# Attention over 16 images: keys' second half, means, values and maxima at other places in slots 0, 2, 4 and 6

## The chip, the cores and the metric

One core of one Trainium2 chip runs the kernel. The metric is the device time of one execution in microseconds (us). TensorE does the matrix products, VectorE (DVE in the rows), ScalarE (ACT) and GpSimd (POOL) the rest; SyncE (SP) issues the transfers.

## The reference

For each of 16 images `x` has 512 channels and 1024 positions. The reference is, without what doesn't matter here:

```python
q, k, v = split(einsum('bchw,oc->bohw', x, w_qkv), 3)   # 8 heads of 64
sim  = einsum('bhdi,bhdj->bhij', q * 64**-0.5, k)
out  = einsum('bhij,bhdj->bhid', softmax(sim), v)
y    = einsum('bchw,oc->bohw', out, w_out) + b_out
y    = y * rsqrt(mean(y*y, axis=channels) + 64**-0.5) * rms_scale
return y + x
```

All of it is in float32. The softmax is over the 1024 keys of each query.

## The kernel before, in words

**Slots and places.** One image is one batch of eight slots (0 to 7). A slot is a pair of heads and one half (512) of the queries. It goes through 16 places (`t`). At the even places TensorE makes the scores of one step of 128 keys for the two heads (`scores`, L741 and L750: four products of 512 columns, two for each head) and ScalarE makes their exponentials (L871). A head has one bank for its scores, so the next step's product of a head waits until the exponential of that head's last step is done (the wait on `prob_ready` in `scores`). The odd places hold everything else. `items_at` lists it: each item has a name and one of four auxiliary banks of PSUM (0 to 3).

**The items.** K0 and K1 are the two halves of the next head pair's keys, each twelve products of 512 columns (L584). ScalarE copies such an item twice (the high parts, L903), and then VectorE subtracts twice (the low parts, L1118), which frees the bank. V0 to V3 are values for later slots (24 products of 256 columns, L628), copied by ScalarE (L913). M00 to M31 are products of keys and queries from which VectorE takes maxima for the next slot (L726, reduced at L1125, L1131 and L1137): `maxima_of_tile` makes tile 0 and 1 at place 1, tile 2 and 3 at place 9; each tile claims banks 0 and 1, then 2 and 3. T transposes the maxima (L642), in the midst of Q, the next queries, at place 15. O0, O1 and P are the projection of the output (L657). R is the mean of squares of the batch before (L666, L667; slots 0 and 1 only): VectorE reads it at L1170.

**Place 9** also holds the values of steps 0 to 3 (`values`, L763, four products a step). `VALUES_FIRST[slot]` says how many of the four steps come ahead of tile 2; tile 3 comes behind all of them.

**Names for what is split.** x is held as a high part, made by ScalarE, and a remainder `x_lo` (`split_x`, L374). An image has eight pieces: 0 to 3 are the first half of the positions, 4 to 7 the second. The next batch's are split in slots 5 and 6. GpSimd makes the remainders of all pieces but number 6; VectorE makes that one at place 4 of slot 6 (`SPLIT_LOW_AT[6] = (6, 4)`, `SPLIT_BY = ((6,), ...)`). In slot 6 the keys are the next batch's. Their item begins with `wait_x(body, h)`: K0 (h = 0) waits for pieces 0 to 3, K1 (h = 1) for all eight, number 6 among them. V1 of slot 6 reads columns of the first half alone.

**Order.** Every engine's order is the order of the program. On VectorE, for each place: the items of the place, then at place 2 the reciprocals (L1183) and the normalisation (L1190), and last the split of x if the place has one. ScalarE makes the exponentials of an even place, then its items. `OUTPUT_HIGH_AT` is the place at which ScalarE makes the high part of the normalised output (L942); in slots 0 and 1 it waits for R, which uses the same buffer. GpSimd adds the exponentials (L1306) and makes the low part of the output at place 8 (L392).

**Ahead of the loop** a prologue (`PRO_ITEMS`) makes the first keys, queries, values and maxima. VectorE copies the mask and the negative identity there (L1246, L1247), ahead of the maxima of tile 1. The first batch has no R; in the last, slots 6 and 7 make no keys, values or queries for a next one.

Of the kernel before, what the change touches and what calls it, by code (L numbers as in the profile page):

```python
# [25 lines left out]

INVERT_SUMS_AT = ((2, 2),) * 8
NORMALISE_AT = (2,) * 8
OUTPUT_HIGH_AT = (4, 8, 8, 4, 8, 6, 4, 4)
OUTPUT_LOW_AT = 4  # L30

REPEAT_K_AT = (8, 9)
# [2 lines left out]
SPLIT_MAXIMA = (1, 3)  # L35


VALUES_FIRST = (2, 1, 0, 0, 0, 1, 2, 0)

# [7 lines left out]
SQUARE_AT = (((7, 14), (7, 14), (0, 0), (0, 0)), ((0, 14), (0, 14), (1, 0), (1, 0)))  # L49
ADD_SQUARES_IN = (0, 1)  # L50
SQUARES_HIGH_AT = ((0, 1), (1, 1))
MEAN_AT = ((0, 3), (1, 7))

INVERT_AT = (((0, 10), (0, 12), (0, 14), (1, 0)), ((1, 10), (1, 12), (1, 14), (2, 0)))
ROOT_AT = ((1, 0), (2, 0))
# [20 lines left out]
def items_at(slot, t, first, last):  # L76

    following = not (last and slot == SLOTS - 1)
    projected = not (last and slot >= SLOTS - SLOT_QUERIES)
    preceding = not (first and slot == 0)  # L80
    out = []
    if t in (1, 9) and following:
        for it in (0, 1) if t == 1 else (2, 3):
            out.append((f"M{it}0", 0))
            if it in SPLIT_MAXIMA:
                out.append((f"N{it}0", 1))
            out.append((f"M{it}1", 2))
    if t == 3 and slot in (0, 2, 4):
        out.append(("K0", 0))
    elif t == 3 and (slot in (1, 3) or slot == 6 and projected or slot == 7 and following):  # L90
        out.append(({1: "V0", 3: "V2", 6: "V1", 7: "V2"}[slot], 0))
    if t == 5 and slot == 6 and projected:
        out.append(("K0", 1))
    elif t == 5 and slot in (2, 4):
        out.append(("K1", 1))
    if LATE_OUTPUT.get(slot - 1) == t:
        out.append(("P", 0 if t == 3 else 2))
    if t == 7:
        if slot == 0:
            out.append(("K1", 1))  # L100
        elif slot in (1, 3):
            out.append((f"V{slot}", 1 if slot == 1 else 3))
        elif slot == 5 and not last:
            out.append(("V0", 3))
        elif slot == 6 and projected:
            out.append(("K1", 2))
        elif slot == 7 and following:
            out.append(("V3", 3))
    if (slot, t) in MEAN_AT and not first:
        out.append(("R", 2))  # L110
    if t == (11 if following else LAST_OUTPUT_AT) and preceding:
        out.append(("O0", 0))
    if t == (13 if following else LAST_OUTPUT_AT) and preceding and slot not in LATE_OUTPUT:
        out.append(("O1", 2))
    if t == 15:
        if following:
            out.append(("T", 0 if slot in LATE_OUTPUT else 2))
        if projected:
            out.append(("Q", 2 if slot in LATE_OUTPUT else 0))
    return out  # L120


def in_halves(slot, name):

    return name == {0: "K1", 1: "V1", 3: "V3", 5: "V0", 7: "V3"}.get(slot)


def output_item(slot, name):
# [26 lines left out]
def body_items(first, last):  # L155
    return [(s, n, k) for s in range(SLOTS) for t in range(PLACES) for n, k in items_at(s, t, first, last)]


def attention_kernel(nc, x, wqkv, wout, bias, scale, consts, out):
# [27 lines left out]
    with ctx:  # L187
# [207 lines left out]
        def output_high_at(body, slot):  # L395
            return LAST_HIGH_AT[slot - SLOTS + 2] if body.last and slot >= SLOTS - 2 else OUTPUT_HIGH_AT[slot]

# [142 lines left out]
        def _(pe):  # L540
# [227 lines left out]
            def one(body):  # L768
                for slot in range(SLOTS):
# [4 lines left out]
                    preceding = not (body.first and slot == 0)  # L774
                    for t in range(PLACES):
                        names = [name for name, _ in items_at(slot, t, body.first, body.last)]
                        if t % 2 == 0:
                            scores(body, slot, t // 2)
# [12 lines left out]
                        elif t == 9:  # L791
                            for j in range(STEPS // 2):
                                if j == VALUES_FIRST[slot] and "M20" in names:
                                    maxima_of_tile(body, slot, 2)
                                if j == 2 and "O0" in names:
                                    item(body, slot, "O0")
                                    item(body, slot, "O1")
                                values(body, slot, j, False)
                            if "M30" in names:
                                maxima_of_tile(body, slot, 3)  # L800
                        else:
                            if t == 5:
                                for name, _ in items_at(slot, 7, body.first, body.last):
                                    if in_halves(slot, name):
                                        item(body, slot, name, part=0)
                            if t == 13 and slot in LATE_OUTPUT:
                                item(body, slot, "Q", part=0)
                            if t == 13 and body.last and slot == SLOTS - 1:
                                values(body, slot, 4, False)
                                values(body, slot, 5, False)  # L810
                                item(Body(epi, B - 1, False, True), 0, "R0")
                            for name in names:
                                if t == 7 and in_halves(slot, name):
                                    item(body, slot, name, part=1)
                                elif name == "Q":
                                    item(body, slot, "Q", (body, slot), 1 if slot in LATE_OUTPUT else None)
                                elif name != "T" or "Q" not in names:
                                    item(body, slot, name)
# [277 lines left out]
        def _(dve):  # L1096
# [103 lines left out]
            def split_w(n, c):  # L1200
                dve.wait_ge(raw_loaded[c], 16)
                ring = w_ring[:, RING_OF[c]].rearrange("p h k n -> p h (k n)")
                dve.tensor_copy(ring[:, 0], raw_at[c]).then_inc(w_hi_set, 1)
                dve.wait_ge(w_hi_set, n + 1)
                dve.tensor_tensor(ring[:, 1], raw_at[c], ring[:, 0].bitcast(F32), ALU.subtract  # L1205
                                  ).then_inc(w_set, 1)
# [34 lines left out]
            for slot, name, k in PRO_ITEMS:  # L1241
                if (slot, name) == (6, "Q"):
                    split_w(2, 1)
                elif (slot, name) == (7, "M10"):
                    dve.wait_ge(const_loaded, 64)
                    dve.tensor_copy(tile_mask[:], raw_mask).then_inc(mask_set, 1)  # L1246
                    dve.tensor_copy(neg_ident[:], raw_ident).then_inc(mask_set, 1)  # L1247
                    dve.wait_ge(mask_set, 2)
                if k is not None:
                    item(start, slot, name)  # L1250
# [178 lines left out]
```

## Time and profile before

| | us |
|---|---|
| median of three runs | 3930.39 |
| lowest, highest | 3929.11, 3931.4 |
| the profiled execution's own time | 3928.97 |
| its span | 3926.7 |
| outside the span | 2.3 |
| TensorE busy in the span | 3890.7 (99%) |
| GpSimd, VectorE, ScalarE busy | 2961.6, 2765.4, 2316.0 |

The page gives busy time of each engine, then the chain of work that ended last, then groups of instructions. A matmul row starts when the engine takes the matmul and ends about 0.2 us after the next has begun, since they are pipelined; the distance between two starts is what one of them costs. In the chain the same work stands with its end instead, so its times lie up to 0.2 us later.

### The profile page before, as it was taken

To read this page: it belongs to the slowest core of one execution; us is meant where nothing else is said; L and a number is where in the kernel's file an instruction comes from. 1 tells how busy PE (TensorE), PEld (TensorE's weight loads), DVE (VectorE), ACT (ScalarE), POOL (GpSimd) and SP (SyncE) were. 2 spreads that over 40 slices of the span, in tenths; PEclk is the share of its full clock that TensorE was granted. 3 is DMA by queue.
4 is the path that set the end of the run, shared out by engine and by line. 5 is a ranking of instruction groups with operands and counts; after the bars stand their busy time and mean duration, and the time that the engine had idled before them with its cause. 6 is when DMAs were issued, how large, how long until landed. Compare 5 with 4: busy or idle time off the path is not lost.

```text
span 3926.7 us, 53756 instructions
## 1 busy us (share of the span) xinstructions
PE 3890.7 (99%) x18650; PEld 2470.0 (63%) x18650; DVE 2765.4 (70%) x2897; ACT 2316.0 (59%) x4057; POOL 2961.6 (75%) x2335
## 2 busy tenths in 40 slices
PE   8999999999999999999999999999999999999998
PEld 5666666666666666666666666666666666666664
DVE  5667676676766777667676776767767676676766
ACT  4556565565655656556565665756657565565564
POOL 6678777787876868777787777877778777787776
PEclk9999999999999999999999999999999999999999
DMA  4111111111111112112021120110201111111110
GB/s 151 48 50 54 44 65 54 44 54 44 68 52 43 64 34 71 49 44 76 22 73 53 37 76 33 65 54 36 73 33 65 54 38 70 45 53 54 38 60 22
DMA packets 71851, 212.24 MB, mean 54 GB/s; under 512 B 8216, under 2 KB 9368, under 8 KB 58784
## 3 DMA queue, kind: packets, MB, share of 16 engines
q1 hardware_dynamic: 71584, 208.80, 15.0%
q8 instruction: 153, 2.51, 0.3%
q14 instruction: 114, 0.93, 0.1%
HBM read 168.92 MB, written 39.85 MB: 53 GB/s over the span
## 4 chain that ended last, share of the span: by engine, by line
PE 94%; DVE 4%; issue 1%; ACT 0%; POOL 0%; DMA 0%; DVEq 0%; POOLq 0%
PE pv L763 24%; PE aux L584 16%; PE score L741 13%; PE score L750 11%; PE aux L628 9%; PE aux L657 8%; PE aux L726 7%; PE pv L682 3%; PE aux L707 2%; DVE inv_sum L1183 1%; DVE k_l L1118 1%; DVE maxima L1125 1%; DVE aux L1131 0%; DVE y_sb L1196 0%; PE aux L642 0%
## 5 line engine op out<-in xcount | busy, mean ns | idle before, releaser
L1306 POOL TENSOR_TENSOR prob_sum<-prob_sum,probs 128x512 f32<-128x512 f32 x1536 | 1953.2, 1301 | 354.7 <-ACT probs L871 354.7
L871 ACT ACTIVATE probs<-score 128x512 f32<-128x512 f32 x2048 | 1111.6, 596 | 786.1 <-PE score L750 779.6
L1125 DVE TENSOR_REDUCE maxima<-aux 128x1 fp32r<-128x1024 f32 x768 | 913.5, 1217 | 357.8 <-PE aux L726 210.0
L763 PE MATMUL pv<-probs,v_sb 128*64 128x512 f32 x4096 | 977.7, 603 | 0.0
L741 PE MATMUL score<-q_hl,k_hh 128*128 128x512 f32 x2048 | 839.5, 410 | 2.3 <-ACT probs L871 2.3
L750 PE MATMUL score<-q_hm,k_l 72*128 72x512 f32 x2048 | 814.4, 398 | 0.5 <-DVE q_hm L1143 0.5
L584 PE MATMUL aux<-x_hi,w_ring 128*128 128x512 f32 x2048 | 656.0, 398 | 7.9 <-DVE x_lo L374 7.1
L1302 POOL TENSOR_TENSOR prob_sum<-probs 128x512 f32<-128x512 f32 x256 | 324.9, 1291 | 356.8 <-ACT probs L871 354.7
L763 PEld LDWEIGHTS pv<-probs,v_sb 128*64 128x64 f32 x4096 | 254.1, 136 | 489.6 <-issue 463.4
L741 PEld LDWEIGHTS score<-q_hl,k_hh 128*128 128x128 f32 x2048 | 387.4, 189 | 167.0 <-issue 90.6
L584 PEld LDWEIGHTS aux<-x_hi,w_ring 128*128 128x128 f32 x2048 | 387.7, 190 | 97.6 <-DVE w_ring L1205 7.0
L1183 DVE RECIPROCAL inv_sum<-inv_sum 128x256 f32<-128x256 f32 x254 | 427.0, 1722 | 8.7 <-ACT inv_sum L934 5.7
L750 PEld LDWEIGHTS score<-q_hm,k_l 72*128 72x128 f32 x2048 | 388.4, 190 | 69.9 <-DVE q_hm L1143 1.1
L584 PE MATMUL aux<-x_lo,w_ring 128*128 128x512 f32 x1024 | 402.5, 393 | 0.0
L1131 DVE TENSOR_REDUCE aux<-aux 128x1 f32<-128x513 f32 x256 | 179.3, 700 | 270.2 <-PE aux L726 269.3
L628 PE MATMUL aux<-w_ring,x_hi 128*128 128x256 f32 x1984 | 363.2, 282 | 0.0
L1143 DVE TENSOR_TENSOR q_hm<-aux,tile_mask 8x512 fp32r<-8x512 f32 x256 | 163.8, 677 | 241.9 <-PE aux L642 241.9
L628 PEld LDWEIGHTS aux<-w_ring,x_hi 128*128 128x128 f32 x1984 | 320.7, 191 | 17.4
L726 PEld LDWEIGHTS aux<-k_hh,q_hm 64*128 64x128 f32 x762 | 116.8, 184 | 300.0 <-issue 246.0
L726 PE MATMUL aux<-k_hh,q_hm 64*128 64x512 f32 x762 | 287.5, 450 | 6.1 <-DVE k_l L1118 3.7
L726 PE MATMUL aux<-k_hh,q_hl 64*128 64x512 f32 x762 | 287.9, 451 | 0.0
L1161 DVE TENSOR_TENSOR y_sb<-y_sb,aux 128x1024 f32<-128x1024 f32 x190 | 230.1, 1211 | 74.1 <-PE aux L657 74.0
(132 smaller groups left out, 5099.9 us busy)
## 6 DMA issues: line engine op xcount, KB each, us to landing
w_ring<-w_split SPq DMA_DIRECT2D x93, 1024.0 KB, 4.8
stage<-x SPq DMA_DIRECT2D x252, 256.0 KB, 5.2
out<-stage SPq DMA_DIRECT2D x124, 256.0 KB, 2.0
w_split<-w_ring SPq DMA_DIRECT2D x3, 1024.0 KB, 11.8
w_split<-y_sb SPq DMA_DIRECT2D x3, 1024.0 KB, 3.9
y_sb<-wqkv SPq DMA_DIRECT2D x4, 512.0 KB, 8.5
probs<-wqkv SPq DMA_DIRECT2D x2, 512.0 KB, 7.3
probs<-wout SPq DMA_DIRECT2D x1, 1024.0 KB, 8.3
```

Source lines behind the costliest of these rows:

```text
L584: last = pe.matmul(out_ap, w[:, wp, k, cols], xp[:, k, xcols], start=(k == 0 and n == 0), stop=(k == KT - 1 and n == 2))
L628: last = pe.matmul(to[:, i * WCOLS:(i + 1) * WCOLS], xp[:, c, jt * P:(jt + 1) * P], w[:, wp, c, :], start=(n == 0), stop=(n == 3 * KT - 1))
L657: last = pe.matmul(bank(k + i), w[:, pair, m * P:(m + 1) * P], o[:], start=(n == 0), stop=(n == 2))
L726: last = pe.matmul(bank(k + h), q_hi_at(nhalf, e, h, it), k_hh[rows, npair % 2, e, h * HALF:(h + 1) * HALF], start=True, stop=True)
L741: pe.matmul(score[e][:], k_hh[:, pair % 2, e, keys], q_hl[:, half, e, :], start=True, stop=False)
L750: pe.matmul(score[e][:], k_l1[0:D + 2 * IT, pair % 2, e, keys], q_hm[0:D + 2 * IT, half, e, :], start=False, stop=True).then_inc(score_rea ...
L763: pe.matmul(pv[half][e * D:(e + 1) * D, :], v_sb[:, pair // 2, j, (pair % 2) * P + e * D:(pair % 2) * P + (e + 1) * D], probs[:, (b * SLOT ...
L871: act.activation(probs[:, step % RING, e, :], score[e][:], ACT.Exp, scale=SOFT).then_inc(prob_ready, 1)
L1125: dve.tensor_reduce(maxima[:, n:n + 1], bank(k, 2), AX_X, ALU.max).then_inc(aux_free[k], 1)
L1183: dve.reciprocal(inv_sum[:, cols], inv_sum[:, cols]).then_inc(inv_ready, 1)
L1302: pool.tensor_tensor(prob_sum[:, e, :], probs[:, (step - 1) % RING, e, :], probs[:, step % RING, e, :], ALU.add).then_inc(prob_added, 1)
L1306: pool.tensor_tensor(prob_sum[:, e, :], prob_sum[:, e, :], probs[:, step % RING, e, :], ALU.add).then_inc(prob_added, 1)
```

## The change

In slot 0, K1 is made whole at place 5 where it was in two halves at places 5 and 7; R moves from place 3 to place 7; the high part of the output moves from place 4 to place 8. In slot 6, K0 moves from place 5 to 3, K1 from 7 to 5, V1 from 3 to 7, with other banks. `VALUES_FIRST` becomes 0 in slots 0 and 6 (from 2) and 1 in slots 2 and 4 (from 0); slots 1, 3, 5 and 7 keep theirs. In the prologue the copies of mask and identity stand ahead of tile 3 of the maxima, not of tile 1.

```diff
-OUTPUT_HIGH_AT = (4, 8, 8, 4, 8, 6, 4, 4)
+OUTPUT_HIGH_AT = (8, 8, 8, 4, 8, 6, 4, 4)
-VALUES_FIRST = (2, 1, 0, 0, 0, 1, 2, 0)
+VALUES_FIRST = (0, 1, 1, 0, 1, 1, 0, 0)
-MEAN_AT = ((0, 3), (1, 7))
+MEAN_AT = ((0, 7), (1, 7))
@@ items_at
-    if t == 3 and slot in (0, 2, 4):
+    if t == 3 and (slot in (0, 2, 4) or slot == 6 and projected):
         out.append(("K0", 0))
-    elif t == 3 and (slot in (1, 3) or slot == 6 and projected or slot == 7 and following):
-        out.append(({1: "V0", 3: "V2", 6: "V1", 7: "V2"}[slot], 0))
-    if t == 5 and slot == 6 and projected:
-        out.append(("K0", 1))
-    elif t == 5 and slot in (2, 4):
+    elif t == 3 and (slot in (1, 3) or slot == 7 and following):
+        out.append(({1: "V0", 3: "V2", 7: "V2"}[slot], 0))
+    if t == 5 and (slot in (0, 2, 4) or slot == 6 and projected):
         out.append(("K1", 1))
...
     if t == 7:
-        if slot == 0:
-            out.append(("K1", 1))
-        elif slot in (1, 3):
+        if slot in (1, 3):
             out.append((f"V{slot}", 1 if slot == 1 else 3))
...
         elif slot == 6 and projected:
-            out.append(("K1", 2))
+            out.append(("V1", 3))
@@ in_halves
-    return name == {0: "K1", 1: "V1", 3: "V3", 5: "V0", 7: "V3"}.get(slot)
+    return name == {1: "V1", 3: "V3", 5: "V0", 7: "V3"}.get(slot)
@@ vector, prologue
-                elif (slot, name) == (7, "M10"):
+                elif (slot, name) == (7, "M30"):
```

## Rows read from the trace of the kernel before

**Rows 1.** The page: busy time of the engines, and the chain's shares.

```profile
PE 3890.7 (99%) x18650; PEld 2470.0 (63%) x18650; DVE 2765.4 (70%) x2897; ACT 2316.0 (59%) x4057; POOL 2961.6 (75%) x2335
PE 94%; DVE 4%; issue 1%; ACT 0%; POOL 0%; DMA 0%; DVEq 0%; POOLq 0%
```

**Rows 2.** Timeline, TensorE, slot 6 of batch 5: start, length, operation.

```profile
1437.16 0.40 PE L628 MATMUL aux<-w_ring,x_hi 128*128 128x256 f32 x2
...
1440.02 0.40 PE L741 MATMUL score<-q_hl,k_hh 128*128 128x512 f32 x1
...
1440.97 0.63 PE L584 MATMUL aux<-x_hi,w_ring 128*128 128x512 f32 x2
```

**Rows 3.** Chain of the same slot: time, length, work; K0's twelve products first.

```profile
1441.13 2.74 PE aux L584 x12
...
1448.51 1.87 PE pv L763 x8
1450.38 0.66 PE aux L726 x3
...
1452.90 0.86 PE aux L726 x4
```

**Rows 4.** Timeline, VectorE, same slot, around piece 6.

```profile
1438.60 3.37 DVE L1183 RECIPROCAL inv_sum<-inv_sum 128x256 f32<-128x256 f32 x2
1442.00 0.69 DVE L1190 TENSOR_TENSOR o_norm<-inv_sum,pv 128x512 f32<-128x512 f32 x1
1442.60 0.68 DVE L374 TENSOR_TENSOR x_lo<-stage,x_hi 128x512 fp32r<-128x512 f32 x1
1444.60 1.39 DVE L1118 TENSOR_TENSOR k_l<-aux,k_hh 64x512 fp32r<-64x512 f32 x2 [1.31 <-ACT k_hh L903]
```

**Rows 5.** Groups by line and form, VectorE's splits of x.

```profile
L374 DVE TENSOR_TENSOR x_lo<-stage,x_hi 128x512 fp32r<-128x512 f32 x19 | 14.0, 743 | 0.6 <-ACT x_hi L986 0.6
```

**Rows 6.** Timeline, TensorE: place 8 of slot 0, place 6 of slot 2.

```profile
1265.88 0.39 PE L741 MATMUL score<-q_hl,k_hh 128*128 128x512 f32 x1
...
1324.47 0.39 PE L741 MATMUL score<-q_hl,k_hh 128*128 128x512 f32 x1
```

**Rows 7.** Timeline, ScalarE, slot 2: copies of K1, then exponentials of place 6.

```profile
1324.67 1.21 ACT L903 ACTIVATE k_hh<-aux 64x512 fp32r<-64x512 f32 x2 [1.38 <-PE aux L584]
1325.91 1.09 ACT L871 ACTIVATE probs<-score 128x512 f32<-128x512 f32 x2
```

**Rows 8.** Timeline, VectorE, slot 2: K1's two subtractions.

```profile
1326.61 1.39 DVE L1118 TENSOR_TENSOR k_l<-aux,k_hh 64x512 fp32r<-64x512 f32 x2
```

**Rows 9.** Timeline, TensorE: tile 2 of the maxima in slot 2.

```profile
1328.14 0.46 PE L726 MATMUL aux<-k_hh,q_hm 64*128 64x512 f32 x1 [0.24 <-DVE k_l L1118]
```

**Rows 10.** Chain of slot 4: tile 2 of the maxima, then four steps of values.

```profile
1388.17 0.88 PE aux L726 x4
1389.06 3.58 PE pv L763 x16
```

**Rows 11.** Windows of L584 alone: us, TensorE busy (instructions), clock, DMA, GB/s.

```profile
36.00:39.40 3.40, 3.30 (x8) 0.51 0.17 70
49.60:53.00 3.40, 2.63 (x13) 1.00 0.61 226
```

**Rows 12.** Windows of the prologue, all engines: busy (instructions), clock, DMA, GB/s.

```profile
44.00:46.20 2.20, 0.65 (x4) 0.37 (x4) 2.20 (x3) 0.36 (x1) 1.62 (x1) 0.99 0.00 0
46.20:49.60 3.40, 3.40 (x9) 2.38 (x10) 2.23 (x3) 1.19 (x2) 0.96 (x1) 0.50 0.75 308
```

**Rows 13.** Timeline, TensorE, prologue: tile 3 of the maxima.

```profile
34.52 0.46 PE L707 MATMUL aux<-k_hh,q_hm 64*128 64x512 f32 x1 [2.49 <-issue]
```

**Rows 14.** Timeline, VectorE, prologue: copies of the mask, tiles 2 and 3.

```profile
26.98 1.23 DVE L1246 CAST tile_mask<-probs 8x1024 bf16<-8x1024 f32 x1
...
32.06 2.36 DVE L1125 TENSOR_REDUCE maxima<-aux 128x1 fp32r<-128x1024 f32 x2 [1.11 <-PE aux L707]
35.26 0.70 DVE L1131 TENSOR_REDUCE aux<-aux 128x1 f32<-128x513 f32 x1 [0.84 <-PE aux L707]
```

## The prediction

> **What bounds the kernel now.** I read the page first. TensorE is busy 99% of the span and carries 94% of the chain that ended last [rows 1]. The other engines have a quarter of the span or more to spare. So a reordering can gain only what TensorE idles or loses at switches between kinds of work, and it can lose whatever new wait it puts ahead of a TensorE instruction. Next I went through the slots of batch 5 with the timeline and the chain, engine by engine: TensorE for the order, VectorE and ScalarE for when an item's bank or input is ready. The other full batches repeat batch 5. What the reader is to see is a stream of products with hardly a hole in it. The holes are at the tiles of the maxima: tile 2 in slot 2 [rows 9], tile 2 in slot 4 [rows 10], tile 3 in slots 0 and 6 [rows 3]. Together they are worth about 1 us a batch, and that is all that this change can win back.
>
> **Slot 6, the step that decides.** The new order is K0 at place 3, K1 at 5, V1 at 7. The amount of work is the same. But K1 begins with a wait for all eight pieces of x, and the remainder of piece 6 comes from VectorE.
>
> When does TensorE want K1? Place 3 begins at 1437.16 and the scores behind it take 0.95 (1440.02 to 1440.97) [rows 2]. K0's twelve products take 2.74 [rows 3]. So TensorE stands at K1 at 1437.16 + 2.74 + 0.95 = 1440.85.
>
> When is piece 6 ready? VectorE is in its reciprocals until 1441.97 and in the normalisation after that. It starts the remainder at 1442.60 [rows 4], which today lies well ahead of K1 at place 7. In the new order K0 is an item of place 3, and the split belongs to place 4, so K0's two subtractions are queued ahead of it. Their inputs are there by then: ScalarE's two copies take 1.21 and start about 0.2 after the last product [rows 6, 7], so they end near 1437.16 + 2.74 + 0.2 + 1.21 = 1441.3. The subtractions take 1.39 [rows 4]: the split runs from 1443.99 to 1444.67. From the end of a VectorE instruction to the TensorE product that it frees there is about 0.14 in slot 2 (1326.61 + 1.39 to 1328.14) [rows 8, 9]. K1 starts at 1444.8. **The new wait is 1444.8 − 1440.85 = 3.95 us.** Queued behind it are all of TensorE's work, and through the scores ScalarE and GpSimd as well. Nothing covers it, since TensorE is the bound. The split is there 19 times, of which four belong to the prologue [rows 5]: 15 batches pay.
>
> Two things go the other way in slot 6. With `VALUES_FIRST` 0 the four steps of values run as one block: 3.58 [rows 10] against twice 1.87 [rows 3], 0.16 less. And tile 3 no longer follows so soon on the reductions of tile 2: 0.86 falls to 0.66 [rows 3], 0.20 less. V1 at place 7 costs nothing more: its bank needs one copy by ScalarE, and slots 3 and 7 already do the same with V3 at place 7 and show no hole. Slot 6: +3.95 − 0.36 = +3.59, times 15 = +53.9.
>
> **The clock.** TensorE doesn't idle for so long anywhere in the loop now. The prologue has the nearest rows. After an idle time of 2.49 with 0.7 us of products behind it [rows 13] the granted clock stood at 0.51, the level of 1.2 GHz, from 36.0 to 39.4. There eight products took 3.30, 0.41 each; at 2.4 GHz thirteen took 2.63, 0.20 each [rows 11]. After 2.2 us with only 0.65 busy it stood at 0.50 for another 3.4 [rows 12]. An idle time of 3.9 us is longer than either. I expect one such stretch behind each stall. A full one costs half of 3.4, or 1.7. Part of some will fall on the idle time itself, where it costs nothing, so I take 1.5. The bounds are 0, if the clock holds, and 3.4, for two full stretches. 15 × 1.5 = +22.5.
>
> The Trainium skill (TensorE: Matmul & The Clock Gate, section "HAM oscillation — how this bites in real kernels") tells of a loop whose every pause sent TensorE back to the half clock, and counts as lost half of the throttled time. By it each stall pays 1.7, as an estimate, and the sum would be 3 us higher. It speaks against this change, since its loss comes on top of the wait. The prologue's rows agree so far.
>
> **Slot 0.** K1 whole at place 5 takes no more time. But only R stands between the scores of place 6 and those of place 8. Place 8 would start at 1265.88 as now, since the same work lies ahead of it [rows 6]. R's two products and the four scores of place 6 take 6 × 0.23 = 1.38 (2.74 for twelve) [rows 3], so K1 ends at 1264.50. In slot 2, K1 is whole at place 5 too and ends at 1324.47. There ScalarE makes K1's copies first (1324.67) and the exponentials of place 6 only at 1325.91 [rows 6, 7]. The first of them takes 0.6 (1.09 for both, overlapping), so it is done 2.04 after K1's end. In slot 0 that is 1266.54, and the scores of place 8 wait for it: +0.70 with the signal. In slot 2 the projection P, three times as long as R, hides this. What was next late would have been tile 2: K1's subtractions end 1326.61 + 1.39 − 1324.47 = 3.53 after K1 has ended in slot 2, but a scaling of 1.8 us that slot 0 doesn't have is ahead of them; without it, copies of 1.21 and a last subtraction of 0.7 make it about 2.3, so 1266.8, then R's reading, about as long as one subtraction, 1267.5. Bank 2 is wanted at 1268.0 now that the scores are late, so this is hidden; with prompt scores it would cost 0.4. Merging the values and the later tile 3 give 0.16 + 0.19 back, as in slot 6. Slot 0: +0.35, times 15 = +5.2. The first batch has no R and waits 1.1 instead: +0.9. ScalarE's later high part of the output, and GpSimd's low part behind it, are wanted only by O0 at place 11. The block of values, 3.58, tile 3 and the scores of place 10 lie between and hide them, so they cost nothing; without that cover O0 would wait for an instruction or two of GpSimd.
>
> **Slots 2 and 4.** One step of values ahead of tile 2 moves it by 1.0 us, past both waits. Slot 2 loses its 0.24 [rows 9] and pays 0.16 for splitting the values: −0.08. Slot 4: 0.88 falls to 0.66 [rows 10, 3], against 0.16: −0.06. Sixteen times both: −2.2.
>
> **Prologue.** The copies, 1.23 for the mask and a little for the identity, say 1.4, now lie under the products of V2 [rows 14]. Ahead of tile 3 they start at 34.42, behind tile 2's reductions, and push the first reduction from 35.26 to 35.8, which the queries of place 15 wait for: +0.5. Bounds 0 and 1.4. In the last batch slot 6 has no keys: −0.2.
>
> **Sum.** 53.9 + 22.5 + 5.2 + 0.9 − 2.2 + 0.5 − 0.2 = +80.6. Against the profiled execution's 3928.97 that is 4009.6. The median of the runs shown stands 1.4 above that execution, so I give 4011 for the median.
>
> **Rivals.**
> - The stall comes and the clock holds: all but the 22.5, 3988.5. For it: I have no row of a single pause amid dense work; both rows are from the prologue, where pauses follow each other. Against: this pause is longer. 0.14.
> - Two half-clock stretches behind most stalls, or slower work on that clock that makes the next item late: 15 × 2.8 instead of 1.5, 4030.5. 0.10.
> - No stall, on the other side. It needs piece 6's remainder ahead of 1440.7 in every batch. The program would have to have it before the reciprocals, or K1 would have to wait only for the pieces of its own products' first rows. Then slot 6 is −0.36 × 15 = −5.4, and the rest +4.2: 3927.8, or 3929 by the median. The point from which it decides is VectorE's order: with the split ahead of the reciprocals there is no wait; behind them, even ahead of K0's subtractions, there are still 2.6 us (1442.60 + 0.68 + 0.14 − 1440.85). Against it stands the order of places in `one`. 0.05.
> - The placement doesn't do what it says in slot 0: tile 2 waits, not the scores. It changes the sum by less than 5 us and lies within the first case.
> - What I don't see: 0.05, above 4031 or between the cases.
>
> **How the numbers follow.** The forecast has 0.66 and its own range is 4003 to 4020 (lost clock of 1.0 to 2.1 a stall, 0.1 us more or less of wait). The range for 8 in 10 adds the rival without the clock's loss and part of the third: 3983 to 4022. A measurement of this kernel can tell about 0.2%, 7.9 us, from no change. Faster needs below 3922.5: 0.02. Within: 0.04, most of it the case without the stall. Slower: 0.94.
>
> **What would show it.** In the changed kernel's slot 6: TensorE idle for 3.7 to 4.0 just ahead of the first L584 of place 5, released by VectorE's x_lo; on VectorE two L1118 between L1190 and L374; a slot 3.6 longer than before, and 5 with the clock's loss; a granted clock of 0.5 for some 3.4 us in each batch. In slot 0, L741 waiting 0.6 to 0.7 for the exponential at place 8. In slots 2 and 4, no idle time ahead of L726. The prediction is wrong if L374 stands ahead of K0's L1118, or if the clock's page shows 1.0 throughout.

## The result, and the profile after

The changed kernel takes 4031.15 us (median of 4 runs, 4029.7 to 4032.53) against 3930.68 for the kernel before on the same chip. The ratio is 1.0256, with a 95% interval of 1.0238 to 1.0274: slower by 100.5 us. The forecast of 4011 had the direction and the place, and missed a fifth of the size. The range ended at 4022.

On the page of the changed kernel TensorE's share falls from 99% to 97% [rows 1]. VectorE and ScalarE do the same work as before.

```profile
span 4027.6 us, 53756 instructions
PE 3924.3 (97%) x18650; PEld 2488.6 (62%) x18650; DVE 2770.3 (69%) x2897; ACT 2316.4 (58%) x4057; POOL 2954.9 (73%) x2335
PE 96%; issue 2%; DVE 1%; ACT 1%; POOL 0%; DMA 0%; ACTq 0%; DVEq 0%; POOLq 0%
```

At the head of the list of TensorE's waits (engine, line, released by: us in total, times, longest) the first entry is new. The second was 2.3 us in 11 waits of at most 0.2 before. The lines of the changed kernel are four lower than before, so L580 is L584 of before, L737 is L741, L370 is L374.

```profile
PE aux L580 <- issue: 62.3, 15, 4.2
PE score L737 <- ACT probs L867: 11.1, 27, 1.0
```

The first comes 15 times, 4.16 each: once in every batch that makes keys for a next one. The profile names no releaser for it ("issue"). TensorE's timeline in slot 6 of batch 5 shows where it lies; this answers [rows 2]:

```profile
1473.11 0.40 PE L746 MATMUL score<-q_hm,k_l 72*128 72x512 f32 x1
1477.66 1.19 PE L580 MATMUL aux<-x_hi,w_ring 128*128 128x512 f32 x2 [4.16 <-issue]
1478.65 0.63 PE L580 MATMUL aux<-x_lo,w_ring 128*128 128x512 f32 x1
...
1482.49 0.63 PE L580 MATMUL aux<-x_lo,w_ring 128*128 128x512 f32 x1
1482.91 0.43 PE L737 MATMUL score<-q_hl,k_hh 128*128 128x512 f32 x1
```

And VectorE's at the same time, which answers [rows 4]:

```profile
1471.12 3.36 DVE L1179 RECIPROCAL inv_sum<-inv_sum 128x256 f32<-128x256 f32 x2
1474.52 0.69 DVE L1186 TENSOR_TENSOR o_norm<-inv_sum,pv 128x512 f32<-128x512 f32 x1
1475.13 1.38 DVE L1114 TENSOR_TENSOR k_l<-aux,k_hh 64x512 fp32r<-64x512 f32 x2
1476.54 1.02 DVE L370 TENSOR_TENSOR x_lo<-stage,x_hi 128x512 fp32r<-128x512 f32 x1
```

The reader is to see two things. K1's first product starts 0.1 us after the remainder of piece 6 ends (1477.56), behind K0's two subtractions. And K1's twelve products then take from 1477.66 to 1482.91, 5.25, where K0's took 2.74 before [rows 3]. The windows of the pause, of K1 and of the two levels of the clock say why (us, then busy of PE, PEld, DVE, ACT, POOL, the granted clock, DMA share, GB/s):

```profile
1473.34:1477.66 4.32, 0.17 (x1) 0.03 (x1) 4.14 (x5) 2.19 (x4) 2.49 (x2) 0.83 0.00 0
1477.66:1482.91 5.25, 5.25 (x12) 4.15 (x13) 0.00 (x0) 0.00 (x0) 0.00 (x0) 0.50 0.00 0
1473.34:1476.17 2.83, 0.17 (x1) 0.00 (x0) 2.78 (x4) 2.19 (x4) 1.65 (x2) 1.00 0.00 0
1476.17:1483.00 6.83, 5.34 (x13) 4.26 (x14) 1.36 (x2) 0.00 (x0) 0.84 (x1) 0.50 0.00 0
```

The clock is still at full level 2.8 us into the pause. It is at half level (1.2 GHz) for 6.8 us, from 1476.17, which is 1.5 before the pause's end, until K1 is done.

Slot by slot for batch 5, from the start of a slot's first score product to the next slot's: slot 6 39.57 where it was 33.07, slot 0 31.13 (30.63), slot 2 31.43 (31.56), slot 4 30.04 (30.10), the others as before. Slot 0's new wait is the second entry of the list. On TensorE's and ScalarE's timelines, as in [rows 6, 7]:

```profile
1297.84 0.40 PE L663 MATMUL aux<-o_lo,ones_c 128*128 128x512 f32 x1
1298.76 0.50 PE L737 MATMUL score<-q_hl,k_hh 128*128 128x512 f32 x1 [0.52 <-ACT probs L867]
1299.10 0.41 PE L746 MATMUL score<-q_hm,k_l 72*128 72x512 f32 x1
1299.34 0.41 PE L737 MATMUL score<-q_hl,k_hh 128*128 128x512 f32 x1
...
1296.87 1.21 ACT L899 ACTIVATE k_hh<-aux 64x512 fp32r<-64x512 f32 x2 [1.38 <-PE aux L580]
1298.11 1.09 ACT L867 ACTIVATE probs<-score 128x512 f32<-128x512 f32 x2
```

### The profile page after: what moved, and what is told of

The parts are those of the page before. It is cut to its first block, busy times and chain, and to the rows that moved or that the text cites. A ratio compares the mean times of both kernels' runs of the same rounds, so it can differ in the third digit from the quotient of the medians.

```text
span 4027.6 us, 53756 instructions
## 1 busy us (share of the span) xinstructions
PE 3924.3 (97%) x18650; PEld 2488.6 (62%) x18650; DVE 2770.3 (69%) x2897; ACT 2316.4 (58%) x4057; POOL 2954.9 (73%) x2335
## 3 DMA queue, kind: packets, MB, share of 16 engines
q1 hardware_dynamic: 71584, 208.80, 14.7%
## 4 chain that ended last, share of the span: by engine, by line
PE 96%; issue 2%; DVE 1%; ACT 1%; POOL 0%; DMA 0%; ACTq 0%; DVEq 0%; POOLq 0%
PE pv L759 23%; PE aux L580 19%; PE score L737 13%; PE score L746 12%; PE aux L624 9%; PE aux L653 9%; PE aux L722 6%; PE pv L678 3%; PE aux L703 2%; ACT probs L867 0%; PE aux L638 0%; ACT k_hh L899 0%; PE pv L624 0%; DVE maxima L1121 0%; PE score L624 0%
## 5 line engine op out<-in xcount | busy, mean ns | idle before, releaser
L737 PE MATMUL score<-q_hl,k_hh 128*128 128x512 f32 x2048 | 842.1, 411 | 11.1 <-ACT probs L867 11.1
L580 PE MATMUL aux<-x_hi,w_ring 128*128 128x512 f32 x2048 | 682.3, 412 | 70.4 <-issue 62.3
L580 PEld LDWEIGHTS aux<-x_hi,w_ring 128*128 128x128 f32 x2048 | 402.1, 197 | 168.7 <-issue 69.8
L737 PEld LDWEIGHTS score<-q_hl,k_hh 128*128 128x128 f32 x2048 | 389.2, 190 | 189.4 <-issue 94.5
L580 PE MATMUL aux<-x_lo,w_ring 128*128 128x512 f32 x1024 | 415.7, 406 | 0.0
L899 ACT ACTIVATE k_hh<-aux 64x512 fp32r<-64x512 f32 x256 | 152.0, 594 | 310.2 <-PE aux L580 307.0
L722 PE MATMUL aux<-k_hh,q_hm 64*128 64x512 f32 x762 | 278.2, 444 | 2.3 <-DVE maxima L1121 1.9
L624 PE MATMUL aux<-w_ring,x_lo 128*128 128x256 f32 x992 | 280.0, 282 | 0.0
```

The lines of the kernel that those rows point to most:

```text
L580: last = pe.matmul(out_ap, w[:, wp, k, cols], xp[:, k, xcols], start=(k == 0 and n == 0), stop=(k == KT - 1 and n == 2))
L624: last = pe.matmul(to[:, i * WCOLS:(i + 1) * WCOLS], xp[:, c, jt * P:(jt + 1) * P], w[:, wp, c, :], start=(n == 0), stop=(n == 3 * KT - 1))
L722: last = pe.matmul(bank(k + h), q_hi_at(nhalf, e, h, it), k_hh[rows, npair % 2, e, h * HALF:(h + 1) * HALF], start=True, stop=True)
L737: pe.matmul(score[e][:], k_hh[:, pair % 2, e, keys], q_hl[:, half, e, :], start=True, stop=False)
```

## The experiments

The theory after the result was: (A) the wait for piece 6 is the one cause, directly and through the clock. Its rivals: (B) the new order of items or banks costs by itself, and (C) K1's slow products have another reason than the clock. Each kernel below was timed beside the kernel before (3929.1 to 3929.9 in these sets).

**1. No wait: piece 6 by GpSimd.** The changed kernel with

```diff
-SPLIT_LOW_AT = ((5, 0), (5, 0), (5, 0), (5, 0), (6, 0), (6, 0), (6, 4), (6, 0))
+SPLIT_LOW_AT = ((5, 0), (5, 0), (5, 0), (5, 0), (6, 0), (6, 0), (6, 0), (6, 0))
-SPLIT_BY = ((6,), (0, 1, 2, 3, 4, 5, 7))
+SPLIT_BY = ((), (0, 1, 2, 3, 4, 5, 6, 7))
```

> The changed kernel, with the remainder of piece 6 of x made by GpSimd behind its pieces 4, 5 and 7 at the start of slot 6, so that K1 at place 5 has nothing to wait for on VectorE. Theory A (the wait for piece 6 and the clock behind it are all of the loss): slot 6 falls from 39.57 us in the changed kernel to 32.7 (33.07 before, less 0.36 for the values and tile 3), slot 0 stays at 31.13, clock 1.00 in the loop, about 3929 us, within 3 of the kernel before. Rival B (V1 at place 7 or the new banks cost by themselves, or GpSimd is late with a fourth piece in slot 6): slot 6 stays above 33.5, 3945 us or more.

Measured: 3929.49, ratio 0.9999 (0.999 to 1.0009). Slot 6 is 32.71, slot 0 31.12. TensorE goes from the scores to K1 without a hole, and GpSimd has the four pieces done at 1439.59, 3.5 us before K1's first product:

```profile
1442.89 0.40 PE L746 MATMUL score<-q_hm,k_l 72*128 72x512 f32 x1
1443.13 0.63 PE L580 MATMUL aux<-x_hi,w_ring 128*128 128x512 f32 x2
...
1434.59 5.00 POOL L370 TENSOR_TENSOR x_lo<-stage,x_hi 128x512 fp32r<-128x512 f32 x4 [2.69 <-ACT x_hi L982]
```

Theory A holds and B falls: of the 100 us none is left. Slot 6's new order, with its block of values and the later tile 3, is even worth 0.36 a batch; slot 0 eats it up.

**2. A shorter wait: piece 6 ahead of K0's subtractions.** The changed kernel with `(6, 2)` for piece 6 in `SPLIT_LOW_AT` instead of `(6, 4)`.

> The changed kernel, with VectorE's split of piece 6 moved from place 4 to place 2, so ahead of K0's two subtractions but behind reciprocals and normalisation. Theory A: the wait falls from 4.2 us idle by 1.4 to 2.8 (the split would end at 14.1 to 14.5 us of slot 6, and K1 is due at 11.64). For the clock there are two expectations: it still falls, for one stretch of 3.4 in most batches, with about 1.2 to 1.5 lost in each: near 3990. Or a pause of 2.6 to 2.8 amid dense work leaves it at 1.00: 3970. Rival B (the wait isn't VectorE's order): no change from 4031.

Measured: 3998.82, ratio 1.0176 (1.0161 to 1.0191). The wait follows VectorE's order, as A says, but the time is above both of its values. The pause was longer than expected, because the remainder took 1.21.

```profile
1467.08 1.21 DVE L370 TENSOR_TENSOR x_lo<-stage,x_hi 128x512 fp32r<-128x512 f32 x1
1468.21 1.38 DVE L1114 TENSOR_TENSOR k_l<-aux,k_hh 64x512 fp32r<-64x512 f32 x2
```

K1's first product comes at 1468.38, 3.1 after it was due, where 2.6 to 2.8 was expected. The clock fell in ten of the 15 batches. By the lengths of slot 6 that cost some 21 us in all, about as much as the 3990 had for it, but not one stretch alike in each batch. Slot 6 of batch 1, of batch 2:

```profile
464.98:500.84 35.86, 32.93 (x159) 21.34 (x158) 22.70 (x25) 19.91 (x35) 23.06 (x19) 1.00 0.09 30
710.41:749.00 38.59, 35.66 (x158) 23.37 (x157) 22.68 (x25) 19.91 (x35) 23.05 (x19) 0.91 0.08 28
```

It is the same pause of 3.1 in both, yet in one the clock never falls and in the other the slot takes 2.7 more (K1's twelve products take 2.83 in one and 5.26 in the other). So the length of a pause alone doesn't settle what follows it.

**3. The wait filled.** The changed kernel with products that nobody uses ahead of the wait:

```diff
+                    if slot == 6 and h == 1 and body.plan is not pro:
+                        for _ in range(18):
+                            pe.matmul(bank(k), w_ring[:, RING_OF[kpair], 0, 0, P:2 * P], x_hi[:, 0, 0:HALF],
+                                      start=True, stop=True)
                     if slot == 6 and body.plan is not pro:
                         wait_x(body, h)
```

> The changed kernel, with 18 products of 512 columns (0.23 each, 4.1 together, their result overwritten) ahead of K1's wait in slot 6, so that TensorE is busy while VectorE finishes piece 6. Theory A (the clock's fall costs 2.5 us in each of 15 batches, because TensorE idles): the granted clock stays at 1.00 in the loop, slot 6 falls from 39.57 to 37.1 although work was added, and the time from 4031 to about 3994. Rival C (K1's slow products have another cause than the clock, or the clock falls anyway): slot 6 stays at 39.6 or grows, 4031 or more.

Measured: 3996.32, ratio 1.0172 (1.0157 to 1.0187), 35 us less than the changed kernel although TensorE does 270 products more. Slot 6 is 37.13. The filling, K1 and the clock over both:

```profile
1465.02 4.29 PE L600 MATMUL aux<-x_hi,w_ring 128*128 128x512 f32 x18
1469.36 0.73 PE L580 MATMUL aux<-x_hi,w_ring 128*128 128x512 f32 x2
...
1472.22 0.39 PE L741 MATMUL score<-q_hl,k_hh 128*128 128x512 f32 x1
...
1464.90:1472.30 7.40, 7.36 (x33) 5.72 (x32) 4.33 (x5) 2.31 (x4) 2.55 (x2) 1.00 0.00 0
```

K1 takes 2.86 at full clock. C falls, all the more since K1 took 2.83 in experiment 2 behind a pause whose clock had held. The 100 us divide into some 65 for the wait itself and the smaller terms, and 35 for the clock.

**4. Slot 6 alone.** The kernel before with slot 6's items, banks and `VALUES_FIRST` of the changed one, and nothing else of it.

> The kernel before with slot 6 alone as in the changed one: K0 at place 3, K1 at 5, V1 at 7, values first 0. Slot 0, slots 2 and 4 and the masks are as before. If slot 6's cost is the same as in the changed kernel (6.50 a batch, 15 times), the time is 3929 + 97.5 = 4026.5. If the clock's loss depends on where its own beat meets the pause, and a batch that is 0.3 us shorter meets it elsewhere, the loss is smaller than 2.5 a batch and the time is 4012 to 4020. If slot 6 is not the cause: 3929 and little more.

Measured: 4030.94, ratio 1.026 (1.0243 to 1.0277). Slot 6 is the cause, but neither number came true. The time is that of the whole change, though slot 0's 0.50 a batch is missing and so are the gains of slots 2 and 4. Slot 6 alone made up for it: 39.88 here against 39.57. The starts of batch 5 and 6 show what stayed the same. First the changed kernel, then this one:

```profile
1282.25 0.40 PE L737 MATMUL score<-q_hl,k_hh 128*128 128x512 f32 x1
1531.42 0.40 PE L737 MATMUL score<-q_hl,k_hh 128*128 128x512 f32 x1
```

```profile
1282.71 0.40 PE L739 MATMUL score<-q_hl,k_hh 128*128 128x512 f32 x1
1531.89 0.40 PE L739 MATMUL score<-q_hl,k_hh 128*128 128x512 f32 x1
```

249.17 and 249.18 us. From batch 3 on, every batch of both kernels lies within 0.1 of 249.15, and from batch 7 on within 0.05. This gave a new theory, L (lock): the instants at which the clock changes its level keep a beat of their own. What a pause costs depends on where in the beat it falls. Each batch's loss moves the next pause, until pause and beat meet at the same place in every batch. From then on the batch's length is set by the beat. Its rival S (sum): each pause costs a fixed amount, and the equal lengths are chance.

The trace of the changed kernel shows the beat itself, in its first batches, which are not yet of equal length. These windows of 0.3 us end and begin where the clock falls, in batch 0 and in batch 1:

```profile
233.42:233.72 0.30, 0.00 (x0) 0.00 (x0) 0.30 (x1) 0.00 (x0) 0.01 (x1) 1.00 0.00 0
233.72:234.02 0.30, 0.00 (x0) 0.00 (x0) 0.26 (x1) 0.00 (x0) 0.00 (x0) 0.50 0.00 0
482.59:482.89 0.30, 0.30 (x3) 0.25 (x2) 0.00 (x0) 0.00 (x0) 0.00 (x0) 1.00 0.00 0
482.89:483.19 0.30, 0.30 (x3) 0.20 (x2) 0.00 (x0) 0.00 (x0) 0.00 (x0) 0.51 0.00 0
```

The falls are 249.17 apart, though the two batches start 246.46 apart. In batch 0 the clock falls ahead of the pause's end, in batch 1 it falls 0.7 after K1 has begun.

**5 and 6. More work, to tell L from S.** The changed kernel with four, and with eight, unused products of 0.23 us ahead of Q in slot 2:

```diff
+                    if slot == 2:
+                        for _ in range(4):
+                            pe.matmul(bank(k), w_ring[:, RING_OF[(slot + SLOT_QUERIES) % SLOTS // 2], 0, 0, 0:P],
+                                      x_hi[:, 0, 0:HALF], start=True, stop=True)
```

> The changed kernel with four more products of 512 columns (0.23 each, overwritten) ahead of Q in slot 2 of every batch, 0.92 us of TensorE's work with nothing beside it. Theory L (lock: the clock changes its level on a beat of its own; the batch has drifted to the place on that beat where pause and loss make it 249.17 us long, as in the changed kernel and in the run with slot 6 alone, whose other work differs by 0.3): the batch stays at 249.17, slot 6 gives back what slot 2 takes, 4031 to 4034. Theory S (sum: every batch loses a fixed 2.5 to 2.9 at the clock): 4031 + 16 x 0.92 = 4046.

> The same with eight products more, 1.84 us a batch. Theory S: 4031 + 16 x 1.84 = 4060. Theory L: the loss would have to fall to about 1.0 for the batch to stay at 249.17. If it can, 4032 to 4036; if the lock ends before that, batches of changing length and 4043 to 4052. In both cases less than the sum.

Measured: four cost 3.3 us in all (4034.47, ratio 1.0265, 1.0251 to 1.0279), eight 21.7 (4052.89, ratio 1.0312, 1.0298 to 1.0326). With four, the products stand in slot 2 at their full price (32.32 for 31.43), and the batch is as long as ever:

```profile
1375.63 1.09 PE L592 MATMUL aux<-x_hi,w_ring 128*128 128x512 f32 x4
...
1286.66 0.40 PE L741 MATMUL score<-q_hl,k_hh 128*128 128x512 f32 x1
...
1535.80 0.40 PE L741 MATMUL score<-q_hl,k_hh 128*128 128x512 f32 x1
...
1482.92:1487.34 4.42, 4.42 (x12) 3.48 (x13) 0.00 (x0) 0.00 (x0) 0.00 (x0) 0.61 0.00 0
```

249.14 from start to start. K1 takes 4.42 instead of 5.25: slot 6 (38.68) gives back what slot 2 took. With eight the loss can't shrink that far. The batches don't settle; they go round in threes of 250.09, 249.80 and 251.07, four starts in a row:

```profile
1291.48 0.40 PE L741 MATMUL score<-q_hl,k_hh 128*128 128x512 f32 x1
...
1541.57 0.40 PE L741 MATMUL score<-q_hl,k_hh 128*128 128x512 f32 x1
...
1791.37 0.40 PE L741 MATMUL score<-q_hl,k_hh 128*128 128x512 f32 x1
...
2042.44 0.40 PE L741 MATMUL score<-q_hl,k_hh 128*128 128x512 f32 x1
```

L's first range (4031 to 4034) was missed by half a microsecond, S's 4046 by 11.5. With eight, 4052.9 is 0.9 above L's second range and 7 below S. S is also at odds with experiment 2, where the same pause cost 0, 1.6 or 2.6 to 2.7. The lock isn't firm: with four products more it held to batch 13, and batch 14 is 249.62 long.

**7. Control for the lock.** Both edits, the 18 products in the wait and the four in slot 2.

> Control for the lock: the run with the wait filled by 18 products, plus the same four products more ahead of Q in slot 2. TensorE never pauses in the loop, so the clock has nothing to give back. Theory L: here the four products cost their full time, 3996.3 + 16 x 0.92 = 4011. If they lie in some slack of slot 2 and that was why they cost 3 us in the changed kernel: 3999.

Measured: 4010.98, ratio 1.0206 (1.0189 to 1.0223): 14.7 above the run with the filled wait, the four products' full price in 16 batches. The same four products cost 3.3 us where TensorE pauses and 14.7 where it doesn't. So L holds for this kernel: the clock's beat is its own, and it sets the length of a batch that has such a pause in it.

**8 and 9. Slot 0 alone; masks alone.** The kernel before with the four edits of slot 0 only; and with `"M30"` for `"M10"` in the prologue only.

> The kernel before with slot 0 alone as in the changed one: K1 whole at place 5, mean at 7, output's high part at 8, values first 0. If the scores of place 8 wait for ScalarE, whose two copies of K1 come ahead of the exponentials of place 6, slot 0 grows by 0.5 in 15 batches and 0.9 in the first: 3937.5, with a wait of 0.7 ahead of L741 at place 8. If the 0.35 a batch of the prediction holds: 3935. If slot 0 pays only within the changed kernel: 3929.

> The kernel before with the copies of mask and identity ahead of tile 3 alone. The prediction had +0.5 us; the trace of the changed kernel, where the two copies end 0.05 us after tile 3's products are there, has +0.1. Both are within what the runs tell apart, so the trace is what counts: idle time of VectorE ahead of the mask's copy, and the start of its first reduction of tile 3 against the end of those products.

Slot 0: 3937.74, ratio 1.0021 (1.0012 to 1.003), 7.8 us. Its list of waits shows the mechanism: 27 waits for the exponentials where the kernel before has 11 of at most 0.2.

```profile
PE score L739 <- ACT probs L869: 10.9, 27, 1.0
```

Masks: 3929.84, ratio 0.9999 (0.9989 to 1.0009), no difference that can be measured. In the changed kernel's prologue the copies end 0.05 before tile 3's reduction begins; this answers [rows 14]:

```profile
34.13 0.68 DVE L1242 CAST tile_mask<-probs 8x1024 bf16<-8x1024 f32 x1
34.74 0.21 DVE L1243 CAST neg_ident<-probs 128x128 fp32r<-128x128 f32 x1
35.00 0.70 DVE L1127 TENSOR_REDUCE aux<-aux 128x1 f32<-128x513 f32 x1
```

**10 and 11. What the change has to give.** First the values alone, `VALUES_FIRST = (2, 1, 1, 0, 1, 1, 1, 0)` in the kernel before. Then slot 6's new order with piece 6 by GpSimd, and `VALUES_FIRST = (2, 1, 1, 0, 1, 1, 0, 0)`, with slot 0 and the masks as before.

> The kernel before with the steps of values alone changed: one ahead in slots 2, 4 and 6 (slot 6 keeps its order of items, whose K1 at place 7 would hold up tile 2 with none ahead). Slots 2 and 4: -0.15 and -0.06; slot 6: the 0.20 at tile 3 goes, 0.0 to 0.1 may come at tile 2's second half. Sum: 3929.1 - 3.2 - 2.2 = 3923.7. If the maxima later by 1 us hold up T or the next slot: 3929 or more.

> What is left when both costs are taken out: the kernel before with slot 6 as in the changed one, piece 6 by GpSimd, and one step of values ahead in slots 2 and 4; slot 0 and the masks as before. By the slots measured: slot 6 32.71 for 33.07 (15 times), slot 2 31.42 for 31.57 and slot 4 30.03 for 30.09 (16 times): 3929.1 - 5.4 - 3.2 = 3920.5. If a slot gives it back elsewhere: 3929.

Measured: 3925.55, ratio 0.9989 (0.998 to 0.9997), and 3921.32, ratio 0.9978 (0.9969 to 0.9987). The second is faster than both kernels, by 8.4 and by 110 us. The first gained 4.1 instead of 5.4, because tile 2's second half waits 0.08 in slot 6 (32.95 instead of 32.87). Slot 6 of batch 5 in the second, without a hole:

```profile
1426.80:1459.50 32.70, 32.70 (x159) 21.41 (x158) 21.57 (x23) 19.91 (x36) 23.85 (x19) 1.00 0.10 33
```

## Why the prediction was right and wrong

| Term | predicted | measured |
|---|---|---|
| wait for piece 6, a batch | 3.95 | 4.32 |
| values and tile 3 in slot 6 | −0.36 | −0.36 |
| clock behind the wait, a batch | 1.5 | 1.5 and 1.6 in the first two, then 2.4 to 2.6 |
| slot 0, a batch | +0.35 | +0.50 |
| slots 2 and 4, together | −0.14 | −0.19 |
| first batch's slot 0 | +0.9 | +0.92 |
| prologue | +0.5 | below 0.1 |
| last batch's slot 6 | −0.2 | −0.34 |
| sum | +80.6 | +100.9 (the two spans) |

**The order of events** was right at each step: where TensorE stands, what VectorE has queued ahead of the split, 15 batches, the half clock behind the pause, the wait for ScalarE in slot 0, the waits that go in slots 2 and 4. The bounds that decided it were simple: an instruction's time, its place in its engine's queue, and when the consumer wants it.

**The clock's term was mis-sized**, and with it the range: 15 × 1.5 = 22.5 stood for what adds up to about 36. The step that failed is "I expect one such stretch behind each stall", 3.4 us of half clock with a part on the idle time, taken from the prologue's two pauses [rows 11 to 13]. The changed kernel has one in its first two batches, which lose 1.5 and 1.6. From the third on two follow each other: in batch 5 the clock is at half level for 6.8 us, 1.5 of them on the pause and 5.3 on products, and 2.5 us are lost. The sign that the prediction named, 0.5 for some 3.4 us in each batch, came in the first two only. Of the 20 us that the sum fell short, 14 are the clock's and 6 the wait's.

The prediction also multiplied one middle value by 15, as if the stalls were independent. Experiments 4 to 7 show that they aren't: each pause meets the clock's beat where the losses before it have put it, until the batches settle. Where they settle depends on the other work: at 2.5 lost in the changed kernel, at 2.9 with slot 6 alone, at 1.65 with four products more. No run tells where another kernel would settle. The rival "two half-clock stretches behind most stalls" had the right mechanism and got 0.10. That its 4030.5 is within 1 us of the result is in part luck: its 15 × 2.8 is a little too much for the clock, and its wait is too short. With no row of a repeated pause in a regular loop, the bound of two stretches should have been in the range.

The Trainium skill (TensorE: Matmul & The Clock Gate, section "Part 1: The HAM clock gate (the "warmup" mystery)") says that the gate's watch on activity runs freely and isn't reset when a kernel starts. The loop agrees: the clock's falls in batches 0 and 1 of the changed kernel are 249.17 apart, though the batches start 246.46 apart. What happens at the kernel's start no run here tests. The Trainium skill (the same page) counts half of the throttled time as lost (section "HAM oscillation — how this bites in real kernels"). K1 comes close to that, 5.25 for 2.77 at full clock in experiment 1, 2.48 lost where half would be 2.63. What follows for a loop, that the loss is neither fixed nor drawn afresh, only the runs above show.

**The wait's 0.37** is mostly the split itself, 1.02 instead of the 0.68 of [rows 4]. It is 1.01 or 1.02 in each of the 15 batches, 1.21 in experiment 2 and 1.09 in experiment 3. These are GpSimd's additions beside it: the second one in the kernel before, the second one in the changed kernel, the first one in experiment 2.

```profile
1442.64 1.79 POOL L1306 TENSOR_TENSOR prob_sum<-prob_sum,probs 128x512 f32<-128x512 f32 x1
```

```profile
1475.75 1.26 POOL L1302 TENSOR_TENSOR prob_sum<-prob_sum,probs 128x512 f32<-128x512 f32 x1
```

```profile
1466.47 1.27 POOL L1302 TENSOR_TENSOR prob_sum<-prob_sum,probs 128x512 f32<-128x512 f32 x1 [1.89 <-ACT probs L867]
```

In the changed kernel GpSimd's addition ends at 1477.01 and VectorE's split at 1477.56; in experiment 2 they end at 1467.74 and 1468.29. The split ends 0.55 behind the addition in both, though it started 0.47 and 0.66 ahead of the addition's end. So it looks as if the split waited for the addition that was under way. In the kernel before, the split started just as one addition ended, took 0.68, and the next addition took 1.79 instead of the usual 1.29: there GpSimd waited. This was read from the rows, and no run of its own tests it.

**Slot 0** waited 0.69 at the first head, as predicted (0.70). The 0.15 that was missed is the second head: its exponential is 0.5 behind the first, and its scores wait a little too, so the four products take 1.15 instead of 1.02.

**The prologue's 0.5** was too much because I took the mask's copy at 1.23 [rows 14]; it took 0.68 at its new place.

## What to carry to other kernels

Before an item moves to an earlier place, list every input that it waits for, and for each the queue of the engine that makes it: here one remainder stood behind two subtractions in VectorE's order, and the wait for it was 4.3 us a batch. A pause of TensorE as long as these can cost the clock as well, and in a loop that repeats the same work this loss can settle at one value. Here that was 1.65, 2.5 or 2.9, and 2.9 is the most that any batch lost; so the range should reach the largest loss that the rows allow. While such a pause is in the loop, the time can't be used to price other edits: four products cost 3.3 us there and 14.7 without it.

## What the runs showed of the hardware that was not expected

- Work added to a loop with a pause in it can cost nearly nothing: 0.92 us a batch more on TensorE left the batch at 249.14 to 249.17, because K1 ran 0.83 faster (4.42 for 5.25) as the half clock covered less of it.
- The clock fell at 233.72 and 482.89, 249.17 apart, in batches that start 246.46 apart. Three kernels with different work settled at the same batch of 249.17 (the third until its batch 13); with 1.84 us more the batches went round in threes of 250.09, 249.80 and 251.07.
- The same pause of 3.1 us in the same loop was followed by no fall of the clock in five of 15 batches (slot 6 35.86) and by 1.6 to 2.7 us of loss in the other ten.
- Unused products that keep TensorE busy through a wait made the kernel 35 us faster than idling through it (3996.32 for 4031.15).
- VectorE's subtraction of 128x512 took 0.68, 1.02, 1.09 or 1.21 beside GpSimd's additions of the same size; in the last three it ended 0.55 behind the addition that was under way when it started.
